# TensorE's plan within a state-space block: single convolution taps, a thinner second layer, and the last sign sum behind its own last scan

## The reference

```python
xc, z = jnp.split(jnp.einsum('btd,ed->bte', x, in_proj_w), 2, axis=-1)
xs = silu(causal_conv(xc, conv_w, 4 taps, per channel) + conv_b)       # 512 channels
dt_r, Bv, C = split(xs @ x_proj_w.T)                                    # 16, 16, 16
dt = softplus(dt_r @ dt_proj_w.T + dt_proj_b)
a = jnp.exp(dt[..., None] * A)                                          # A = -exp(A_log), 16 states
u = dt[..., None] * Bv[:, :, None, :] * xs[..., None]
_, h = jax.lax.associative_scan(_affine_combine, (a, u), axis=1)        # h_t = a_t h_(t-1) + u_t
y = (jnp.einsum('btis,bts->bti', h, C) + xs * D_skip) * silu(z)
attn = y @ out_proj_w.T

h = s0 * ([x, -x] @ sign(k0)); h = relu(h) * 2                          # 256 -> 1024
h = s1 * (h @ sign(k1));       h = relu(h) * 2                          # 1024 -> 1024
ffn = s2 * (h @ sign(k2))                                               # 1024 -> 256
out = x + attn + ffn                                                    # of the normed x
```

## Time and profile before

| | |
|---|---|
| median of 3 runs | 3686.15 us (3685.03 to 3688.43) |
| the profiled execution | 3683.52 us, its span 3681.7 us |
| TensorE (matmuls) busy | 3381.3 us, 92% |
| VectorE busy | 2735.0 us, 74% |
| ScalarE busy | 2217.7 us, 60% |
| GpSimd busy | 1501.7 us, 41% |
| granted clock of TensorE, mean | 0.96 |
| state-space phase | from about 2480 us on, its first scan at 2514.25 us |

### The profile page before, as it was taken

One profiled execution on the slowest core, in us unless ns is written; L12 is line 12 of the kernel. 1 busy time (PEld: TensorE's weight loads), 2 busy tenths in 40 slices (PEclk: granted clock), 3 DMA queues, 4 the chain that ended last, 5 costly groups with the idle time before them and its releaser, 6 DMA issues. The chain is left out here.

```text
span 3681.7 us, 61156 instructions
## 1 busy us (share of the span) xinstructions
PE 3381.3 (92%) x20658; PEld 1448.4 (39%) x20671; DVE 2735.0 (74%) x4434; ACT 2217.7 (60%) x3461; POOL 1501.7 (41%) x1849
## 2 busy tenths in 40 slices
PE   8996999989999999999999999677998998989987
PEld 5563666643333333333333333342333333333332
DVE  4653223458888888888888888256888888888888
ACT  3331221137777777777777777637667766667663
POOL 2212000013333333323323333206778777777776
PEclk9997999989999999999999999888999999999988
DMA  4443111111111111111111010131212212222221
GB/s 152 143 138 98 46 44 44 41 37 39 48 41 30 32 34 33 33 33 33 30 33 31 28 29 25 37 120 58 73 60 79 66 65 71 65 75 70 64 72 52
DMA packets 159225, 211.69 MB, mean 57 GB/s; under 512 B 30659, under 2 KB 106699, under 8 KB 158939
## 3 DMA queue, kind: packets, MB, share of 16 engines
q1 hardware_dynamic: 142042, 174.47, 15.5%
q10 hardware_dynamic: 10752, 16.78, 1.4%
q0 software_dynamic: 6144, 16.79, 1.4%
HBM read 154.48 MB, written 52.69 MB: 56 GB/s over the span
## 5 line engine op out<-in xcount | busy, mean ns | idle before, releaser
L1331 DVE TENSOR_REDUCE pmax<-psR 128x1 f32<-128x512 f32 (+3 forms) x2170 | 1318.3, 669 | 162.0 <-PE psR L1383 94.5
L1277 ACT ACTIVATE prob<-psS 128x1024 f32<-128x1024 f32 (+3 forms) x1280 | 1099.9, 905 | 339.7 <-PE psS L1436 331.9
L2091 POOL TENSOR_TENSOR hc<-h_d,crep 128x512 f32<-128x512 f32 x512 | 649.0, 1272 | 253.6 <-DVE h_d L2305 203.3
L1383 PE MATMUL psR<-kslab,qslab 48*128 48x512 bf16 (+3 forms) x2480 | 677.3, 353 | 45.1 <-DVE pmax L1331 20.3
L1436 PE MATMUL psS<-qslab,kslab 51*128 51x512 bf16 (+3 forms) x2560 | 643.6, 352 | 6.8 <-ACT prob L1277 4.4
L1451 PE MATMUL psVo<-prob,vaug 128*32 128x512 f32 (+3 forms) x5120 | 625.4, 544 | 0.9 <-ACT ov L1281 0.9
L1209 POOL TENSOR_SCALAR_AFFINE_SELECT prob<-prob 128x256 f32<-128x256 f32 (+1 forms) x512 | 209.0, 421 | 779.6 <-ACT prob L1277 779.2
L2305 DVE TENSOR_TENSOR_SCAN h_d<-a,state,psU 128x512 f32<-128x512 f32 x384 | 489.3, 1274 | 0.0
L2295 DVE TENSOR_TENSOR psU<-dtx,psX 128x512 f32<-128x512 f32 x512 | 356.1, 695 | 165.6 <-PE psX L2449 102.7
L1383 PEld LDWEIGHTS psR<-kslab,qslab 48*128 48x128 bf16 x2480 | 185.3, 94 | 720.3 <-DVE pmax L1331 532.5
L2213 ACT ACTIVATE a<-dt,a_neg 128x512 f32<-128x512 f32 x512 | 364.7, 720 | 54.4 <-DVE h_d L2305 53.1
(11 more groups left out here) (289 smaller groups left out, 4852.8 us busy)
## 6 DMA issues: line engine op xcount, KB each, us to landing
crep<-c_rows_d SPq DMA_DIRECT2D x256, 256.0 KB, 3.2
x_e<-rows_d SPq DMA_DIRECT2D x72, 128.0 KB, 2.0
y_d<-y SPq DMA_DIRECT2D x72, 128.0 KB, 1.7
q_d<-parts SPq DMA_DIRECT2D x48, 128.0 KB, 2.4
k_d<-parts SPq DMA_DIRECT2D x48, 128.0 KB, 4.4
qslab<-q_d SPq DMA_DIRECT2D x64, 96.0 KB
kslab<-k_d SPq DMA_DIRECT2D x64, 96.0 KB
x<-in_L_attn_x_dram SPq DMA_DIRECT2D x8, 512.0 KB, 6.1
```

What stands on the lines that cost most here:

```text
L1277: act.activation(prob[g % BUFS][:, :, off:BLK], psS[g % 2][:, :, off:BLK], ACT.Exp).then_inc(prob_ready, 1)
L1331: dve.tensor_reduce(pmax[:, a].rearrange("p i c -> p (i c)")[:, lo:lo + (count - 1) * NEXT + 1:NEXT], psR[at % BANKS][:, 0:count * w].rear ...
L1383: ins = pe.matmul(dst[:, m * w:(m + 1) * w], qslab[u][rows, i * P:(i + 1) * P], kslab[u][rows, ch * BLK:ch * BLK + w], start=(m == 0), sto ...
L2091: pool.tensor_tensor(hc[:, g % CR], h[:, g % HR], crep[:, g // PAIR % SPR], ALU.mult).then_inc(hc_ready, 1)
```

## The change

Three things change in the plan of a block and in the readers that follow it.
- The convolution of group c takes one tap in each of four units (from units 17, 23, 28 and 33) where it took two taps in each of two (from 20, 24, 28, 32).
- The second layer's items 1 to 3 take four units each (5, 4, 4, 3 products, from 22, 27 and 32) where they took three; items 4 to 7 come at 37, 41, 45 and 49 where they came at 34, 38, 42 and 46. Around them `l1` 4 and 5, `xz` 2 to 7, `xd`, `dt` and `l3` move by a few units. The second `l3` item ends in unit 62.
- VectorE reads the second `l3` item in unit 63 of its own block, behind the last scan.

```diff
--- before.py
+++ after.py
@@ -1899,7 +1899,7 @@
                     done += count
                 assert done == OPS[kind]
 
-            for f, at in enumerate((0, 2, 4, 6, 10, 13, 15, 17)):
+            for f, at in enumerate((0, 2, 4, 6, 9, 12, 15, 17)):
                 put("l1", f, at, [4])
             for c in range(PAIR):
                 put("dt", PAIR + c, 1 + 2 * c, [1])
@@ -1907,18 +1907,20 @@
                 put("out", 0, 8, [2, 2, 2, 2])
                 put("out", 1, 13, [2, 2, 2, 2])
             put("l2", 0, 18, [4, 4, 4, 4])
-            for f in range(1, FT):
-                put("l2", f, 18 + 4 * f, [6, 5, 5])
-            put("l3", 0, 52, [6, 6, 5, 5, 5, 5])
-            put("l3", 1, 58, [6, 6, 5, 5, 5, 5])
+            for f in range(1, 4):
+                put("l2", f, 17 + 5 * f, [5, 4, 4, 3])
+            for f, at in enumerate((37, 41, 45, 49)):
+                put("l2", 4 + f, at, [6, 5, 5])
+            put("l3", 0, 53, [6, 7, 6, 7, 6])
+            put("l3", 1, 58, [7, 6, 7, 6, 6])
             if blk + 1 < NBLK:
-                for e, at in enumerate((5, 7, 12, 16, 49, 51, 53, 55)):
+                for e, at in enumerate((5, 7, 10, 14, 48, 52, 56, 60)):
                     put("xz", e, at, [2])
-                for c in range(CT):
-                    put("cv", c, 20 + 4 * c, [2, 2])
-                put("xd", 0, 36, [2, 2])
-                for c in range(PAIR):
-                    put("dt", c, 41 + 4 * c, [1])
+                for c, at in enumerate((17, 23, 28, 33)):
+                    put("cv", c, at, [1, 1, 1, 1])
+                put("xd", 0, 38, [1, 1, 2])
+                for c, at in enumerate((44, 46)):
+                    put("dt", c, at, [1])
             return plan
 
         ALL = NBLK * UNITS
@@ -2100,12 +2102,12 @@
                 if blk + 1 < NBLK:
                     if t in (31, 33):
                         cut_x(blk + 1, (t - 31) // 2)
-                    if t in (40, 42):
-                        rest(blk + 1, (t - 40) // 2)
-                    if t in (51, 53):
-                        step_size(blk + 1, (t - 51) // 2)
+                    if t in (42, 44):
+                        rest(blk + 1, (t - 42) // 2)
                     if t in (52, 54):
-                        scaled_input(blk + 1, (t - 52) // 2)
+                        step_size(blk + 1, (t - 52) // 2)
+                    if t in (53, 55):
+                        scaled_input(blk + 1, (t - 53) // 2)
 
         @block.scalar
         def _(act):
@@ -2259,17 +2261,17 @@
                 if t == 7:
                     log_term(blk, 1)
                 if blk + 1 < NBLK:
-                    if t in (27, 35):
-                        silu_conv(blk + 1, (t - 27) // 8)
+                    if t in (28, 38):
+                        silu_conv(blk + 1, (t - 28) // 10)
                     if t == 19:
                         copy_x(blk + 1)
-                    if t in (39, 41, 43):
-                        cut_bc(blk + 1, (t - 39) // 2)
-                    if t == 47:
+                    if t in (41, 43, 45):
+                        cut_bc(blk + 1, (t - 41) // 2)
+                    if t == 49:
                         log_exp(blk + 1, 0)
-                    if t == 48:
+                    if t == 50:
                         log_term(blk + 1, 0)
-                    if t == 57:
+                    if t == 62:
                         silu_gate(blk + 1)
 
         @block.vector
@@ -2340,8 +2342,8 @@
                 if g + 1 < ALL:
                     input_term(g + 1)
                 scan(g)
-                if t == 1 and blk:
-                    sign_out(blk - 1, 1)
+                if t == UNITS - 1:
+                    sign_out(blk, 1)
                 if t == LAG and blk:
                     gate(blk - 1, 1)
                 if t == SEG + LAG:
@@ -2354,7 +2356,6 @@
                             sign_out(blk, e)
                         if kind == "out":
                             add_out(blk - 1, e)
-            sign_out(NBLK - 1, 1)
             gate(NBLK - 1, 1)
             for j in range(2):
                 add_out(NBLK - 1, j)
```

## The result

The kernel after takes 3648.21 us, the median of four runs (3644.86 to 3649.81); the kernel before, run beside it, 3685.77 us (3685.03 to 3688.43). The ratio is 0.9896, 95% interval 0.9882 to 0.991: 37.6 us less, where 34 was forecast (3652, range 3634 to 3676). Beside the experiments the kernel before had medians of 3685.4 to 3687.0 us, so a difference between two kernels that ran on different chips is good to a few us only. One execution of one experiment (`e10_xz_back`) took 6521 us and is left out of its figures.

The account below looks back on a forecast made before the run. VectorE, needing 132 us a block, was held to 146.8 by waits for TensorE's spread. The terms summed to -5.1 us in each of blocks 1 to 6, -35 with the outer blocks, giving 3652 us after rounding, range 3634 to 3676.

Parts of the forecast that it names:

- rival 1: Whole kernel: the forecast itself, 3638 to 3666 us, chance 0.61.
- A: Block starts: sign sum behind the last scan shortens TensorE's 5.56 us wait to about 2, saving 3.8 us a block.
- B: Units 18 to 39, convolutions and second layer: TensorE's excess over VectorE falls to 2.3 us, saving 6.6 us a block.
- C: Units 9 to 16: moved first-layer and input-projection items make spreads late, costing 1.9 us a block (0 to 3.4).
- D: Units 38 to 51: the deferred second layer brings 1.0 us of new waits a block (0 to 2).
- E: Clock: new TensorE buffer waits bring half-clock stretches at block starts and unit 9, costing 2.4 us a block (0 to 6.8).
- 2 (better): ScalarE is early enough and the clock holds, a block saving 9.4 us: 3626 to 3638 us, chance 0.11.
- 3: The clock falls at unit 17 too, +3.4 us in six blocks: 3672 us (3666 to 3679), chance 0.14.
- 4: Units 22 to 41: groups wait for psW buffers, bringing back 6 us a block: 3686 us, chance 0.06.
- 5: Gaps at units 9 and 17 each bring 13.65 us at half clock under full load: 3719 us, chance 0.08.

Follow-up runs that it names:

- e10_xz_back: Kernel after with only input-projection items 2 and 3 put back to units 12 and 16: 3659.36 us, ratio 0.9926.
- e3_front_as_before: Kernel after with l1 items 4 and 5 and xz items 2 and 3 back where they stood before the change: 3628.73 us, ratio 0.985.
- e1_sign_alone: Kernel before with only the sign sum moved behind its own block's last scan and the second l3 item ending in unit 62: 3659.89 us, ratio 0.9932.
- e4_taps_in_pairs: Kernel after with each convolution again in two units of two taps (from 18, 24, 29, 34): 3641.65 us, ratio 0.9878.
- e7_front_and_pairs: Kernel after with l1 4 and 5, xz 2 and 3 as before the change and convolutions in two units of two taps: 3619.40 us, ratio 0.9823.
- e5_spread_repeated: Kernel after with the spread in each block's unit 2 made eight times more, same data and result: 3640.37 us, ratio 0.9877.
- e6_l1_item_back: Kernel after with only first-layer item 4 put back from unit 9 to unit 10: 3643.22 us, ratio 0.9886.
- even plan: Kernel after with the whole table laid anew, each pair's products fitted into 3.99 us and bank readers in time: 3580.29 us, ratio 0.9713.
- e2: Kernel after with the sign sum back in unit 1 of the next block, the second l3 item still ending in unit 62: 3668.84 us, ratio 0.9954.

## Why the prediction was right

The forecast (rival 1) came out: 3648 against 3652, all of its parts with the right sign. (Its sum gives 3650 to 3651; it was rounded up.) By its steps, in us a block, with the clock kept apart as the prediction keeps it, that is, from blocks that lost nothing to it:

- **A**, forecast -3.8, measured -4.8: TensorE's wait for the sign sum fell from 5.56 to 0.57, with 1.77 behind it, and the waits of the gate and of the terms beside it went. Units 0 to 17 fell from 42.84 to 37.62 (blocks 1 and 2 of `e3_front_as_before`), and the sum itself cost 0.45 at the end. With the clock's share in it, `e1_sign_alone` measured -3.7. The forecast counted no gain behind unit 8, where the old start had made TensorE late.
- **B**, forecast -6.6: right in place and mechanism, units 18 to 39. In `e3_front_as_before`, which leaves the front out, they take 50.31 against 55.79: -5.5; in the kernel after 49.27: -6.5. The excess of 2.3 us that the forecast left is what the waits there come to (0.93 + 0.22 + 0.71 + 0.22 and the gate's 0.85, less 5 x 0.12). That the splitting of the taps helps is the one part of the picture that fell (`e4_taps_in_pairs`, `e7_front_and_pairs`). The rest of B's cause is what these runs leave over; no run has the thinner second layer alone.
- **C**, forecast +1.9, measured +1.4 (139.4 against 138.0 in `e3_front_as_before`). Right, for the reason given: first-layer item 4 waits for ScalarE's copy (2.21 us in block 3 and 2.39 in the others, 2.3 forecast), and in blocks 2, 3 and 6 the waits for the terms of units 12, 14 and 18 are 0.5 to 1.0, 1.0 and 1.3 us (0.8, 0.8 and 1.1 forecast). The wait for the spread of unit 18 stayed, as said (1.44, was 1.35). The price of the front on the medians is 19.5 us; on the spans it is 17.9, of which six blocks are 13.3 with the clock's part in them, blocks 0 and 7 1.9 and the start of the phase, which the front cannot touch, 2.8.
- **D**, forecast +1.0: units 40 to 51 take 1.3 longer, in the three waits shown.
- **E**, forecast +2.4, measured +1.7, the term furthest off for its size. Blocks 1 and 5 took 3.0 and 5.1 us more than 139.4, block 4 some 1.7 more than its own time without the clock (an estimate, from `e5_spread_repeated`: 139.85 less the 1.7 of its one stretch), the others 0.5 together; 10 us in six blocks. The forecast had a start in six of ten blocks at 2.0 and unit 9 in one of three at 3.4. Measured were all six starts at 1.4 on the mean, and one unit 9 of six at 1.7, since every stretch there lasted 3.41 us and not 6.8. The reading that waits below 1.5 us cost no clock fell too: 1.49 us in block 4 was followed by 6.83 us at half.
- Sum: -4.8 - 5.5 + 1.4 + 1.3 + 1.7 = -5.9, forecast -5.1. By the table's columns: -4.29 + 3.17 + 0.90 - 7.42 + 1.32 + 0.45 = -5.9. That the total came within 1 us a block owes something to luck: A gave 1.0 more than forecast and E and C cost 1.2 less, while B gave 1.1 less.

Of the rivals, 2 (better) needed ScalarE early at unit 9, which it was not. 3: the gap of 1.56 to 2.03 us at unit 17 never brought the clock down in blocks 1 to 6 (once each in `e5_spread_repeated` and `e6_l1_item_back`, in block 3, for 3.41 us). 4: in units 22 to 39 of blocks 1 to 6 TensorE stands idle nowhere for as much as 0.25 us, so nothing there waits for a bank. 5: full-load units ran at half clock once, for 3.41 us, not for 15 us a block.

What stays open: why the clock gave way at unit 9 in block 5 and not in four others with the same 2.39 us of idle ahead; and how far the medians' 7.8 us of `e5_spread_repeated` are the clock at starts, since the profiled executions differ by 3.8.

## What to carry to other kernels

When two engines hand over at nearly equal work (here 132 and 130 us a block), count the waiting one's idle time and ask where the other's queue exceeds the pace in a window as short as the buffers allow; a plan laid by this rule, with the sign sum moved as here, gave 105 us (3685.4 - 3580.3), where this change gave 38. An item whose reader works in the next stage's first units holds a buffer over the boundary: let it be read behind the stage's own last step (26 us here alone, some 16 to 19 in the even plan). Buffers dealt out by order of ends make moves non-additive, so try moves together and not one by one.

## What the runs showed of the hardware

- The clock's fall did not go by the length of the idle time alone. In blocks 1 to 6 of the kernel after, idle times of 1.49 to 1.99 us at the starts were each followed by half clock (six of six); 2.39 us at unit 9 was in one of five; 1.56 to 2.03 us at unit 17 in none of six. In the even plan's block 0, 2.18 and 1.40 us within 6 us left it at full.
- Nor did it go by the place. Six kernels have the same idle time at the starts (after, `e3`, `e4`, `e6`, `e7`, `e10`): it was followed by half clock in 31 of 36 blocks (in one of them only 5 us later), and not, for one, in block 1 of `e3`, `e4`, `e6` and `e7`, with 1.99 us. The 2.2 to 2.4 us at unit 9 were in 9 of 30 (after, `e2`, `e4`, `e5`, `e10`). The 2.3 to 2.5 us at the moved input-projection item of `e10_xz_back` were in six of six. What decides is not shown; that TensorE's pairs hold little work at the starts may be a part of it (argued, not tested). That eight products in the gap are enough there, `e5_spread_repeated` shows, but not whether the filled gap or the work added does it.
- What a half-clock stretch costs goes by where it lies: 3.41 us cost 1.7 at units 9 and 17 and 0.1 to 0.2 at a block's start; 10.24 us at the start of block 1 cost 3.0.
- More TensorE work made the kernel faster: 64 products of 0.22 us more, 7.8 us less.
- An f32 product behind f16 ones and ahead of the spread costs 0.87 us, ahead of the f32 sum of states 0.95.
- The time at which the phase begins differs by up to 8.3 us between profiled executions (2513.52 to 2521.81) though nothing ahead of it was changed, so a difference of a few us between two spans need not be one of the phase.
